# First mixture and second self attention of a two-layer block in one stage, by halves of four batches

## The reference, cut to what matters

```python
    x = x + _L0_ffn_ref(_layernorm(x, axis=-1), ...)   # first mixture
    x = x + _L1_attn_ref(_layernorm(x, axis=-1), ...)  # second self attention

        # _L0_ffn_ref: 16 experts of width 128, 8 chosen for each position, and a shared one
        hg = jnp.einsum('bsd,eid->bsei', x, w_gate)
        hu = jnp.einsum('bsd,eid->bsei', x, w_up)
        h = jax.nn.silu(hg) * hu
        ye = jnp.einsum('bsei,edi->bsed', h, w_down)
        y = jnp.einsum('bsed,bse->bsd', ye, combine).astype(x.dtype)

        # _L1_attn_ref: 16 heads of 8 features; head h sees each STRIDES[h]-th position
        STRIDES = [1, 1, 2, 2, 2, 2, 4, 4, 4, 4, 8, 8, 8, 8, 16, 16]
            for h, stride in enumerate(STRIDES):
                k_s = k[:, h, ::stride, :]
                v_s = v[:, h, ::stride, :]
                scores = jnp.einsum('bqd,bkd->bqk', q[:, h], k_s) * scale
                attn = jax.nn.softmax(scores, axis=-1)
                outs.append(jnp.einsum('bqk,bkd->bqd', attn, v_s))
        attn_out = hepos_attention(x, Wqkv, bqkv, Wout, bout)
        h = layer_norm(x + attn_out, gamma, beta)
        ffn = jax.nn.relu(h @ W1 + b1) @ W2 + b2
        return layer_norm(h + ffn, gamma, beta)
```

## Time and profile before

| | us |
|---|---|
| median of 3 runs (588.16 to 593.43) | 591.06 |
| the profiled execution | 592.91 |
| its span | 590.9 |
| TensorE busy in it | 529.3 |

### The profile page before, as it was taken

How to read it: one execution, slowest core, us unless ns; L and a number is a source line. 1 busy time by engine, 2 the same in 40 slices (tenths; PEclk the granted TensorE clock), 3 DMA queues, 4 the chain that set the end, 5 groups by cost and what they waited for, 6 DMA issues and landing times. The chain is left out here.

```text
span 590.9 us, 10213 instructions
## 1 busy us (share of the span) xinstructions
PE 529.3 (90%) x3367; PEld 370.6 (63%) x3367; DVE 376.1 (64%) x887; ACT 334.3 (57%) x759; POOL 213.7 (36%) x236
## 2 busy tenths in 40 slices
PE   3989998998799997999979999796899987999996
PEld 1556675676356655888855668362466654777774
DVE  3388878778367625566653177736567457788875
ACT  1566776776257725456536065121376445889883
POOL 2677821000345630665631900103002372354510
PEclk9999999999799998999998599797899987999998
DMA  5722300000000000444402000000200001112101
GB/s 183 199 70 71 91 15 1 2 1 1 2 2 1 1 2 12 167 125 131 127 16 54 1 2 0 0 1 10 63 1 3 0 2 37 36 42 66 36 0 35
DMA packets 23456, 23.74 MB, mean 40 GB/s; under 512 B 3418, under 2 KB 17556, under 8 KB 23316
## 3 DMA queue, kind: packets, MB, share of 16 engines
q1 hardware_dynamic: 22560, 22.58, 13.2%
q10 hardware_dynamic: 852, 0.60, 0.4%
HBM read 22.56 MB, written 0.61 MB: 39 GB/s over the span
## 5 line engine op out<-in xcount | busy, mean ns | idle before, releaser
L1863 DVE TENSOR_TENSOR e_h_lo<-e_h,e_h_hi 128x512 fp32r<-128x512 f32 x60 | 47.8, 825 | 17.5 <-ACT e_h_hi L1724 17.4
L1128 POOL TENSOR_TENSOR e_gc<-e_g,e_c 128x512 f32<-128x512 f32 x32 | 41.9, 1312 | 42.1 <-ACT e_g L1111 22.8
L1720 ACT ACTIVATE e_h<-e_h,m_b 128x512 f32<-128x512 f32 x64 | 43.7, 688 | 10.9 <-PE e_h L1621 10.9
L544 ACT ACTIVATE a_p<-a_s,a_m 128x128 f32<-128x128 f32 x128 | 49.4, 390 | 0.0
L852 ACT ACTIVATE x_pT<-x_turn 77x1024 f32<-77x1024 f32 x32 | 32.5, 1017 | 17.9 <-PE x_turn L795 17.9
L1087 ACT ACTIVATE e_h_hi<-e_h 128x512 fp32r<-128x512 f32 x34 | 21.5, 632 | 34.3 <-DVE e_h L1170 26.1
L1176 DVE TENSOR_TENSOR e_h_lo<-e_h,e_h_hi 128x512 fp32r<-128x512 f32 x34 | 23.8, 699 | 26.0 <-ACT e_h_hi L1087 25.3
L1724 ACT ACTIVATE e_h_hi<-e_h 128x512 fp32r<-128x512 f32 x64 | 38.5, 631 | 0.0
L795 PE MATMUL x_turn<-consts,x_p 128*77 128x128 f32 x256 | 35.1, 281 | 1.8 <-ACT x_pT L852 1.8
L795 PEld LDWEIGHTS x_turn<-consts,x_p 128*77 128x77 f32 x256 | 29.1, 151 | 9.8 <-issue 7.3
L1762 POOL TENSOR_TENSOR m_w_hi<-m_w,e_one 128x512 fp32r<-128x512 f32 x16 | 19.0, 1186 | 43.2 <-PE e_y L1621 26.2
(11 more groups left out here) (301 smaller groups left out, 1459.0 us busy)
## 6 DMA issues: line engine op xcount, KB each, us to landing
e_c<-spread SPq DMA_DIRECT2D x32, 256.0 KB, 3.2
m_w<-in_L_ffn_W SPq DMA_DIRECT2D x16, 256.0 KB, 3.1
a_raw<-in_experts SPq DMA_DIRECT2D x17, 192.0 KB, 2.4
a_wkv<-in_L_attn_Wkv SPq DMA_DIRECT2D x2, 512.0 KB, 6.4
a_reversed<-scratch SPq DMA_DIRECT2D x4, 256.0 KB, 5.4
a_pick_f<-in_pick SPq DMA_DIRECT2D x1, 768.0 KB
x_all<-in_x SPq DMA_DIRECT2D x2, 256.0 KB, 5.3
a_wq<-in_L_attn_Wq SPq DMA_DIRECT2D x1, 512.0 KB, 6.5
```

The lines of the kernel that those rows point to most:

```text
L544: done = act.activation(p[g % 3][:, h, :], s[g % 3][:, h, :], ACT.Exp, bias=m[g % 3][:, h:h + 1], accum_out=r[g % 3][:, h:h + 1])
L1128: pool.tensor_tensor(gc[k % 2][:, :], g[u % 2][:, :], c[k % NC][:, :], ALU.mult).then_inc(S["weighted"], 1)
L1720: act.activation(h[half][f], hb[f][:, :], ACT.Gelu, bias=b1[j][:, f:f + 1]).then_inc(S["gelu_done"], 1)
L1863: dve.tensor_tensor(h_lo[half][f][:, :], h[half][f], h_hi[half][f][:, :].bitcast(F32), ALU.subtract).then_inc(S["lo_done"], 1)
```

## The change

`mixture0`, `attention1` and both norm stages become one stage, `mixture0_attention1`; the second cross attention follows it at once. Its parts are placed by numbers: in the mixture by the unit `u` (with `Z` = 22), after it by the step `n` of the softmax (16 steps, of 384 and of 336 key columns, two for each batch; the list of steps runs on to 29).

```diff
@@ PE, mixture units, then steps @@
-            y_turned(1)
+                if u == Z + 6:
+                    xn_turned(0)
+                if u == Z + 7:
+                    queries(0)
+                if u == Z + 8:
+                    keys_of(0)
+                if u == Z + 9:
+                    values_of(0, range(0, HB))
+                if u >= N + 1:
+                    attention_step(u - N - 1)
+            for n in range(LAG - 1, END):
+                attention_step(n)
@@ PE, one step @@
+            def attention_step(n):
+                if n < STEPS:
+                    scores_of(n)
+                if 1 <= n <= STEPS:
+                    weights_turned(n - 1)
+                if 2 <= n <= STEPS + 1:
+                    weighted_values(n - 2)
+                if n == 2:
+                    y_turned(1)
+                if n == 4:
+                    xn_turned(1)
+                if n == 5:
+                    queries(1)
+                    keys_of(1)
+                if n == 6:
+                    values_of(1, range(HB, B))
+                for h_ in range(2):
+                    k = n - BETA[h_]
+                    if k == 1:
+                        outputs_turned(h_)
+                        projected(h_)
+                    if k == 4:
+                        h_turned(h_)
+                        up(h_)
+                    if k == 5:
+                        back_down(h_)
+                    if k == 8:
+                        next_turned(h_)
@@ ACT, one step (DVE's: with_out at k == 2, with_down at 6) @@
+                if n == 4:
+                    xT_out(1, 2)
+                if n == 5:
+                    q_out(1)
+                    keys_out(1, range(0, 2))
+                if n == 6:
+                    keys_out(1, range(2, HG))
+                    repeated_out(1)
@@ DVE, step k == 7 of half 0 @@
+                    dve.wait_ge(S["scaled"], 2)
+                    own_values(dve.tensor_tensor(half_of(x_all, 0), half_of(x_all, 0), half_of(y, 0), ALU.add))
+                    statistics(x_all, 0)
@@ POOL, both norms of half 0 and its next norm (half 1: the powers and one addition) @@
+            def tail(h_, k):
+                ys, hs, ns = half_of(y, h_), half_of(hh, h_), half_of(xn_all, h_)
+                rstd_of(k, h_)
+                if h_ == 0:
+                    pool.wait_ge(S["n_rstd"], k)
+                    own_values(*normalised(0, y, y))
+                    own_values(pool.tensor_tensor(ys, ys, row(gamma), ALU.mult))
+                    pool.tensor_tensor(hs, ys, row(beta), ALU.add).then_inc(S["h_ready"], 1)
...
+                rstd_of(k + 1, h_)
+                if h_ == 0:
+                    pool.wait_ge(S["n_rstd"], k + 1)
+                    own_values(*normalised(0, y, y))
+                    pool.tensor_tensor(ys, ys, row(gamma), ALU.mult).then_inc(S["scaled"], 1)
+                rstd_of(k + 2, h_)
+                if h_ == 0:
+                    pool.wait_ge(S["n_rstd"], k + 2)
+                    for ins in normalised(0, x_all, xn_all):
+                        ins.then_inc(S["xn_done"], 1)
```

More of the change, by code:

```diff
@@ new lines, in scores_of @@
+            def scores_of(n):
+                b, of = divmod(n, 2)
+                if n == 0:
+                    pe.wait_ge(S["gated"], N)
+                    pe.wait_ge(S["made"], N)
+                if n >= 2:
+                    pe.wait_ge(S["shifted"], n - 1)
+                pe.wait_ge(S["q_out"], b // HB + 1)
+                pe.wait_ge(S["keys_out"], HG * (b // HB + 1))
+                order = OF_STEP[of] if of == 0 else [OF_STEP[1][k] for k in (0, 2, 4, 1, 3, 5)]
+                for tile, h0, nh, stride, _, to, at in order:
+                    row = slice(32 * tile, 32 * tile + 32)
+                    j = h0 % HG
+                    width = nh * (P // stride)
+                    moving = keys[row, b, j:j + nh, :] if stride == 1 else keys[row, b, j:j + nh, 0:P:stride]
+                    mm = pe.matmul(bank[to][:, at:at + width], q[row, P * b:P * b + P], moving, start=True, stop=True)
+                mm.then_inc(S["scores_done"], 1)
@@ L1541, in mixture1 @@
+                    statistics(x_all, 0)
+                if u == Z + 2:
+                    normalise_x(range(0, 2), 1)
+                if u == Z + 3:
+                    normalise_x(range(2, HB), 1)
+                if u == N - 1:
+                    values_masked(0)
+            for n in range(END):
+                attention_step(n)
 def mixture1(nc, a, tools, cross_attention, x_all, xn_all, xnT_all, consts, tables):
```

723 lines of the change are left out of this document (376 added, 347 removed).

## The result

The changed kernel takes 638.3 us (median of 4 runs, 638.0 to 639.8) against 591.1: ratio 1.081, 95% interval 1.077 to 1.084. Forecast were 606 and a range of 591 to 622. The sign was right; the time is 32 us above the forecast, a loss of 47 us where 15 were forecast.

The account below looks back on a forecast made before the run. PE was taken to bound the mixture's second half and end the softmax loop's waits. Rebuilding 304.1 to 411.9 with a serial tail behind POOL gave +15.4 us on 592.9: 608.3 profiled, 606 as median, range 591 to 622.

Parts of the forecast that it names:

- The mechanism of the tails: After the first statistics: PE's in-order queue waits for POOL's norm chain (7.0 us first), tails run serially; 598 to 614, chance 0.60.
- C: Half 0's tail, from its first statistics to its last turns and copy: 35.3 us, to 393.5.
- D: Half 1's tail, its first turns standing behind half 0's last: 31.7 us, to 425.2; 32.0 with the stage's end of 0.3.
- the signs named beforehand: What the new profile would show from the first scores to the cross attention: times, waits, clock and order of products.
- Two signs: First scores near 312, and PE waiting about 4 us for POOL ahead of half 0's turns.
- term B: From the first scores to half 0's first statistics: 45.9 us, with 13 softmax steps and half 1's preparation.
- 3.8 a batch. I take 3.7: Softmax loop: the round from one shift to the next of that kind is 3.8 us; 3.7 taken, 13 steps 24.0.
- rival 3: Softmax loop: the clock falls and stays, nothing filling PE's stalls; 9 to 14 us more, 615 to 620; chance 0.17.
- Term A: Work put into the mixture's second half: 8.2 us, including 0.8 for ACT and DVE; first scores at 312.3.
- Term E: Second cross attention's start after some 10 us without PE work: first two products 3.7 instead of 1.95, 1.8 us more.
- Clock terms of C, D, E: Tails and cross attention: if the clock never falls, C loses 2.5 us, D 3.9 and E 1.8.
- the upper bound's +8: Values before and in the loop: at 2.1 a batch, half 1's at half clock of that, +8 us, 614.

Follow-up runs that it names:

- e2: Changed kernel with DVE's division of a batch's outputs ahead of the next softmax shift instead of behind it; 631.6 us, ratio 1.071.
- e11: e6 with scores as in the kernel before: keys masked by head, two wide 128-row products a batch, not ten of 32 rows; 621.1 us, ratio 1.051.
- e10: e6 with each score product on all 128 rows of queries and keys instead of its 32 (output not the reference's); 625.7 us, ratio 1.058.
- e1: Changed kernel plus two to eight filling products a step in softmax steps 2 to 14, ahead of the weighted values; 648.6 us, ratio 1.098.
- e6: e2 plus one block of 14 filling products in step 7, ahead of that step's weighted values; 631.3 us, ratio 1.071.
- e12: e11 without the block of filling products; 625.1 us, ratio 1.058.
- e5: Changed kernel with DVE's half 0 addition, statistics and norm spread over six mixture units, between each unit's two recurring operations; 631.0 us, ratio 1.067.
- e14: e13 plus 16, 12 and 20 filling products ahead of three sets of turns in the tails; 612.6 us, ratio 1.032.
- e13: Changed kernel with the edits of e2, e5 and e7, half 0's tail norms on DVE instead of POOL, and the wide scores of e12; 612.1 us, ratio 1.038.
- e7: Changed kernel with half 0's turns and up products behind the last scores, its last turns behind half 1's projection; 629.6 us, ratio 1.068.
- e15: e14 plus a block of ten filling products in step 7 behind half 1's values; 616.2 us, ratio 1.039.

## Why the prediction came out short

**What held.** The mechanism of the tails: POOL's chain took 7.0 as summed, half 1's values 6.5, C 37.1 for 35.3, D 33.5 for 32.0. One part of C is right by luck: PE comes to half 0's turns 7 us after the statistics, as summed, but for its own slow queue and not for POOL. Of the signs named beforehand, a clock under 0.7 behind the second values, scores 15 behind the up products, POOL scalings of 0.8 and L1175 behind L1217 are there. PE did wait for ACT ahead of those values, 1.33 us, not 3.1. Two signs failed: the first scores stand at 317.0 and not near 312, and PE's wait for POOL ahead of half 0's turns, about 4 us, wasn't there (e2, faster by then, waits 2.04).

**The step that failed is term B's "3.8 a batch. I take 3.7".** Measured are 8.0, and 65.3 for the sum of 45.9, 19.4 more. The sum of the work was sound: at full clock a batch with wide scores takes 3.8 us (e11), one with e10's high products 4.5 (358.28 to 362.80). What was missing is a term for the clock in the loop, which I put at nothing, and one wait.

- The clock, about 15 us. I priced turns, weighted values and scores at the old loop's 0.99. I had this as rival 3 (the clock falls in the loop itself, 0.17) but with the wrong cause: I reasoned that stalls without fillers would do it, for four to six batches, 9 to 14 us. e1 shows 0.50 without any stall, e6 shows the loop's products lower a clock that was just raised, and e10 that the same loop with its scores on 128 rows doesn't. It holds for all batches, at 6.5 us each even with no wait (e2). With wide scores half 0's statistics stand 51.4 us after the first scores (e12) instead of 60.9 (e2), so 9.6 of the 15 hang on the form of the scores. The last 5.4 or so e12 still has, with half the loop at 0.50 behind half 1's values. Half 1's queries and keys, 1.8 in the sum, took 3.7 at that clock (338.41 to 342.08). I had noticed that the new scores have another shape and priced only their duration ("scores 1.2 to 1.8").
- The wait for `o_normed`, 4.4 us (e2). The kernel before has two output banks; the new one has one. This stood in the code of the change, as did the place of `outputs` behind `softmax_shift`.

**Term A**, 6.0 short from the mixture's start, had 0.8 as an allowance for DVE and ACT. The new norm on DVE stands behind `low_part`, in a ring where a unit waits for DVE: 4.5 us (e5). The table's 4.7 are fewer by luck, as the mixture began 1.3 us earlier. **Term E** had the first two products, right to the tenth, and forgot the 18 fillers behind them, 2.5 us. **Clock terms of C, D, E:** 8.2 us were put on the clock of the waits; filling them gave 2.4 in the stretch (e14). My reading, not tested, is that the chain of statistics, power, scaling and turns itself bounds the tails: behind e14's fillers PE still waits 3.27 and 4.79 us for it.

**Two slips in the working.** Turns and weighted values by their rows are 0.9 + 1.6 = 2.5 us a batch, not 2.2; nothing hangs on it, since the round of 3.8 was taken. And the upper bound's +8 doesn't hold half 1's values "at half clock of that": the rows have 1.94 for 1.16 at full clock, so 2.1 becomes 3.5 a batch, 14.0 for four instead of 6.5, and with half 0's 3.4 the bound is +10.9, about 617. Measured are 638.

**The rule that I weighed.** The Trainium skill, "TensorE: Matmul & The Clock Gate", section "HAM oscillation", puts the fall on gaps of idle PE. I held the row of the values against it, rightly; but I did not carry the same row over to the loop. Here e1 (PE busy for 15.00 of 15.00 us at 0.50) and e6 (the clock falls with PE busy for 5.00 of 5.00) speak against the rule as the only cause. Other rows agree with it: in e10, between 317 and 338, waits of up to 1.20 us left the clock at 1.00, and behind the wait of 3.19 it was 0.50.

**What stays open.** Why the clock is 0.50 with half 1's values, which have 128 rows and few columns, wasn't separated from their width by a run of its own; nor was the part that the narrow weighted values have in keeping it down in e12. And e13 is 21 us slower than the kernel before for reasons that I only argue: from half 0's statistics (363.4) to the cross attention (428.1) its two tails take 64.7 us, largely one behind the other, where the old stage, with both halves interleaved, takes 45.5 from the end of the loop (366.4 to 411.9).

## What to carry to other kernels

When a change gives TensorE's products another shape, price the clock with the shape: in this case a stage full of products on few rows ran at half clock without any idle time, and its other products took twice as long too. Where a stage is cut into halves to overlap, look for what each in-order queue finds next: of a wait of 14.6 us won at one place (e7) 10.7 returned at the next. And split a difference of a few microseconds by stages before you believe it; three of them here came from 18 fillers far behind the edit, and up to five from where the mixture began, far ahead of it.

## What was not expected of the hardware

- The granted clock at 0.50 for 30 us with PE busy all the time (e1), and at 1.00 with it idle for a quarter of 23 us (e10, 317 to 340). e6 and e10, which differ in nothing but the height of the score products, 32 against 128 rows, are at 0.50 and 1.00 behind the same block.
- A block of 14 filling products lifted the clock within 5.6 us (e6, no wait ahead of it) and 5.9 us (e11, behind a wait of 2.54). A block of ten, 4.45 us behind a wait of 2.53, did not (e15), while the ten of the kernel before stood right behind busy values and were followed by wide scores and a clock of 0.99.
- Two scalings of 128 columns took 1.57 us on DVE beside POOL's work (0.78 each), against 1.11 for four without it (0.28 each).
- Products on 32 rows at full clock: 12 records in 0.72 us (e6, 392.14), against 1.50 on 128 rows (e10). They save time and cost the clock.
